# Attention scores of a decoder kernel as eight products of 32 rows and 64 queries in two waves of four, with the keys spread by ScalarE

## The reference

```python
sim = einsum('bghnd,bhsd->bghns', q, k) / scale          # attn0
scores = einsum('bhqd,bhkd->bhqk', Q, K) / sqrt(hd)      # attn1
scores = where(causal, scores + slopes * rel, -inf)
u = einsum('hbqd,hbkd->hbqk', q, k) * scale / sqrt(d_k)  # cross1
logits = tanh(u) * exp(log_C)
```

## Time and profile before

| | us |
|---|---|
| median of 3 runs | 2997.16 (2996.25 to 3002.15) |
| the profiled execution, its own time | 3003.07 |
| span of the profiled execution | 3001.2 |
| TensorE busy (matmul) | 2651.9 (88% of the span) |
| VectorE busy | 2357.9 (79%) |
| ScalarE busy | 1901.2 (63%) |
| GpSimd busy | 1133.4 (38%) |
| mean granted TensorE clock | 0.939 of full speed |

### The profile page before, as it was taken

One profiled execution on the slowest core, in us unless ns is written; L12 is line 12 of the kernel. 1 busy time (PEld: TensorE's weight loads), 2 busy tenths in 40 slices (PEclk: granted clock), 3 DMA queues, 4 the chain that ended last, 5 costly groups with the idle time before them and its releaser, 6 DMA issues.

```text
span 3001.2 us, 97587 instructions
## 1 busy us (share of the span) xinstructions
PE 2651.9 (88%) x36618; PEld 1996.7 (67%) x36618; DVE 2357.9 (79%) x6371; ACT 1901.2 (63%) x3499; POOL 1133.4 (38%) x965
## 2 busy tenths in 40 slices
PE   2999953867888888888899998999989999999998
PEld 2666632546777777777566665666767777777776
DVE  7999999777899999998699998666676666666665
ACT  1777752545566666665466665666667777777776
POOL 0333344008899999998233222444230000000000
PEclk9999975977999999999899999999789999999999
DMA  5000000000000000000100000000000000000000
GB/s 160 1 0 0 0 15 0 1 0 3 1 0 0 0 0 0 0 0 0 58 0 0 0 0 3 16 16 16 7 1 1 1 14 0 0 14 0 14 0 14
DMA packets 28702, 26.67 MB, mean 9 GB/s; under 512 B 4304, under 2 KB 23504, under 8 KB 28496
## 3 DMA queue, kind: packets, MB, share of 16 engines
q1 hardware_dynamic: 28624, 25.63, 2.9%
HBM read 21.43 MB, written 4.19 MB: 9 GB/s over the span
## 4 chain that ended last, share of the span: by engine, by line
PE 82%; DVE 9%; issue 5%; DVEq 1%; ACT 1%; POOL 1%; DMA 0%; ACTq 0%; POOLq 0%; SPq 0%
PE ps L1070 8%; PE ps L896 8%; PE ps L1059 5%; PE ps L1186 5%; PE ps L919 4%; PE ps L934 4%; PE ps L907 4%; PE ps L1084 4%; PE ps L1188 4%; PE ps L1155 4%; PE ps L1187 4%; PE ps L1157 4%; PE ps L1156 4%; DVE work L1612 3%; PE ps L947 2%
## 5 line engine op out<-in xcount | busy, mean ns | idle before, releaser
L470 POOL TENSOR_TENSOR work<-work,consts_sb 128x1024 f32<-128x1024 f32 x192 | 365.0, 1901 | 751.2 <-ACT work L602 590.1
L1070 PEld LDWEIGHTS ps<-work 32*32 32x32 f32 x16384 | 244.0, 145 | 122.9 <-issue 121.2
L1070 PE MATMUL ps<-work 32*32 32x32 f32 x16384 | 249.8, 226 | 72.6 <-DVE work L1612 59.5
L1755 DVE TENSOR_TENSOR h_low<-consts_sb,h_up 128x1024 fp32r<-128x1024 f32 x128 | 158.2, 1236 | 188.2 <-ACT h_up L797 188.2
L722 ACT ACTIVATE ps<-work 128x128 f32<-128x128 f32 x512 | 154.6, 354 | 232.0 <-DVE work L1594 220.9
L896 PE MATMUL ps<-work 128*128 128x512 f32 x512 | 262.4, 614 | 3.1 <-issue 0.2
L1186 PE MATMUL ps<-h_low,d_up 128*128 128x512 f32 x512 | 214.4, 419 | 0.6 <-DVE h_low L1755 0.5
L1155 PE MATMUL ps<-a_low,w_up 128*128 128x512 f32 x512 | 203.4, 397 | 0.9 <-DVE a_low L1730 0.9
L1188 PE MATMUL ps<-h_up,d_low 128*128 128x512 f32 x512 | 200.4, 391 | 0.0
L1157 PE MATMUL ps<-a_up,w_low 128*128 128x512 f32 x512 | 200.4, 391 | 0.0
L1156 PE MATMUL ps<-a_up,w_up 128*128 128x512 f32 x512 | 200.3, 391 | 0.0
(11 more groups left out here) (270 smaller groups left out, 6889.8 us busy)
## 6 DMA issues: line engine op xcount, KB each, us to landing
ctxT_all<-in_ctxT SPq DMA_DIRECT2D x1, 4096.0 KB, 12.9
work<-in_ctx SPq DMA_DIRECT2D x64, 64.0 KB, 1.8
out<-x_all SPq DMA_DIRECT2D x4, 1024.0 KB, 5.1
big<-in_up SPq DMA_DIRECT2D x1, 2048.0 KB, 8.4
consts_sb<-in_consts SPq DMA_DIRECT2D x1, 936.0 KB
w<-in_key_inT SPq DMA_DIRECT2D x1, 512.0 KB, 3.9
w<-in_key_out SPq DMA_DIRECT2D x4, 128.0 KB, 4.0
rows_sb<-in_rows SPq DMA_DIRECT2D x1, 384.0 KB
```

The costliest lines, as they stand in the source:

```text
L470: pool.tensor_tensor(KX[:, u].rearrange("p g (h k) -> p g h k", h=PER_SET), KC[:, u].unsqueeze(2).to_broadcast([P, SETS, PER_SET, SEQ]), o ...
L1070: ins = pe.matmul(psW[rows, n // 16, :, n % 16], XT[rows, T.u, :, n], YT[rows, T.u, :, n], start=True, stop=True)
L1755: dve.tensor_tensor(h_low[:, n], hid[n], h_up[:, n].bitcast(F32), ALU.subtract).then_inc(h_split, 1)
```

## The change

The 128 channels are now four strips of 32 rows with four heads each. A score product takes one strip's 32 rows and the 64 queries of one sequence, against 256 columns: four heads by 64 keys, where `KX[:, u, j, :]` is k with all but head j of each strip zeroed. `quarter_scores` issues four of them as a wave; wave 0 takes strips 0 and 2, wave 1 strips 1 and 3, so that two strips with the same output partitions write banks 0 and 1; wave 1 waits for a semaphore that wave 0 raises. The queries are one plain [128, 128] block (`QT`) with no zero blocks. q and k are each one product of 128 columns, q is copied in one piece, and `spread_k` makes `KX` on ScalarE straight from PSUM in four passes whose scale and bias columns are `own` (1 for the pass's head, else 0) and `own_bk`. GpSimd spreads only in cross1, half as many columns. In attn0 the bias of v enters by two products of one row, and ScalarE copies v; in attn1 VectorE still does. In cross1 the queries are turned by one transpose and copied by VectorE, and the keys are copied from the turned context that is in SBUF already (`cT`). Banks are dealt out anew, the order lists of the three stages are rewritten, and the statistics of x wait on a semaphore in place of a drain.

```diff
-        QB = carve(2 * SETS * P).rearrange("p (u g c) -> p u g c", u=2, g=SETS)
-        KC = carve(2 * SETS * SEQ).rearrange("p (u g k) -> p u g k", u=2, g=SETS)
-        KX = carve(2 * HEADS * SEQ).rearrange("p (u g n) -> p u g n", u=2, g=SETS)
+        QT = carve(2 * P).rearrange("p (u c) -> p u c", u=2)
+        KT = carve(2 * P).rearrange("p (u c) -> p u c", u=2)
+        KX = carve(2 * PER_ROWG * P).rearrange("p (u j c) -> p u j c", u=2, j=PER_ROWG)
...
-        psA, psOT = bank(4, 0), bank(4, P)
-        psQ = bank(4, 2 * P, SETS * SEQ).rearrange("p (g c) -> p g c", g=SETS)
-        psKc = bank(5, 0, SETS * SEQ).rearrange("p (g c) -> p g c", g=SETS)
-        psKd = bank(2, 0, SETS * SEQ).rearrange("p (g c) -> p g c", g=SETS)
-        psV, psY = bank(6, 0), bank(6, P)
+        psA = bank(4, 0)
+        psQ = dict(attn0=bank(4, P), attn1=bank(5, 0))
+        psK = dict(attn0=bank(5, 0), attn1=bank(6, P), cross1=bank(5, 0))
+        psV = dict(attn0=bank(6, 0), attn1=bank(6, 0))
+        psY = dict(attn1=bank(4, P), cross1=bank(6, 0))
+        psOT = dict(attn1=bank(7, 2 * P), cross1=bank(4, 0))
```

The spreading, before and now:

```diff
+            def spread(T):
+
+                pool.wait_ge(aT_ready, T.now(NORM["cross1"]))
+                need(pool, sT_done, T.before(2))
+                pool.tensor_tensor(KX[:, T.u], KT[:, T.u].unsqueeze(1).to_broadcast([P, PER_ROWG, P]),
+                                   own[:, :].unsqueeze(2).to_broadcast([P, PER_ROWG, P]), ALU.mult).then_inc(kx_ready, 1)
...
+            def spread_k(name):
+                base = ATTN[name]
 
                 def seg(T):
                     act.wait_ge(k_done, T.now(base))
-                    need(act, kx_ready, T.before(2, base))
-                    for g in range(SETS):
-                        ins = act.activation(KC[:, T.u, g, :], psKc[:, g, :], ACT.Identity, bias=bk_s[:, g:g + 1])
...
-            def copy_q(base):
+                    need(act, s_done, T.before(2, base))
+                    for j in range(PER_ROWG):
+                        ins = act.activation(KX[:, T.u, j, :], psK[name], ACT.Identity, scale=own[:, j:j + 1], bias=own_bk[:, j:j + 1])
+                    ins.then_inc(kx_ready, 1)
+                return seg
+
...
+                    need(act, s_done, T.before(2, base))
+                    act.activation(QT[:, T.u, :], psQ[name], ACT.Identity, bias=bq_s[:, 0:1]).then_inc(qb_ready, 1)
+                return seg
...
+                    for h in range(2):
+                        part = slice(SEQ * h, SEQ * h + SEQ)
+                        ins = act.activation(VBp[part, T.u, :, :, h, 0:DH], psV[name][part, :].rearrange("p (b i d) -> p b i d", b=2, i=PAIRS),
+                                             ACT.Copy)
+                    ins.then_inc(vb_ready, 1)
+                return seg
```

TensorE:

```diff
+                    if name == "attn1":
+                        pe.wait_ge(kx_ready, T.ahead(1, base, NT))
+                    pe.sem_inc(pe_seen, 1)
+                    if bias is not None:
+                        for h in range(2):
+                            side = slice(SEQ * h, SEQ * h + SEQ)
+                            pe.matmul(to[side, :], ones[SEQ * h:SEQ * h + 1, 0:SEQ], bias[SEQ * h:SEQ * h + 1, :], start=True, stop=False)
                     for b in range(2):
                         for h in range(2):
-                            ins = pe.matmul(psV[SEQ * h:SEQ * h + SEQ, SEQ * b:SEQ * b + SEQ], aT[:, T.u, SEQ * b:SEQ * b + SEQ],
-                                            w[:, SEQ * h:SEQ * h + SEQ], start=True, stop=True)
+                            ins = pe.matmul(to[SEQ * h:SEQ * h + SEQ, SEQ * b:SEQ * b + SEQ], aT[:, T.u, SEQ * b:SEQ * b + SEQ],
+                                            w[:, SEQ * h:SEQ * h + SEQ], start=bias is None, stop=bias is None or b == 1)
                     ins.then_inc(v_done, 1)
...
+            def rows_of(g):
+                return slice(BLOCK * g, BLOCK * g + BLOCK)
+
+            def quarter_scores(u, wave, start):
+
+                at = PER_ROWG * SEQ * wave
+                for n in range(SETS):
+                    for b in range(2):
+                        rows, part = rows_of(SETS * n + wave), slice(SEQ * b, SEQ * b + SEQ)
+                        ins = pe.matmul(ps[part, n, at:at + PER_ROWG * SEQ].rearrange("p (j k) -> p j k", j=PER_ROWG), QT[rows, u, part],
+                                        KX[rows, u, :, part], start=start, stop=start or wave == 1)
+                return ins
+
+            def scores(base, causal, wave):
+
+                def seg(T):
+                    if wave == 0:
                         pe.wait_ge(qb_ready, T.now(base))
                         pe.wait_ge(kx_ready, T.now(base))
-                    need(pe, less_max, T.step(SETS, g + 1 - SETS, base))
-                    if causal:
-                        pe.matmul(ps[:, g, :], maskq_b[0:MASK_ROWS, :], maskk_b[0:MASK_ROWS, g, :], start=True, stop=False)
-                    pe.matmul(ps[:, g, :], QB[:, u, g, :], KX[:, u, g, :], start=not causal, stop=True).then_inc(s_done, 1)
-                return seg
-
-            def scoresT(base):
-
-                def seg(T):
-                    u = T.u
-                    pe.wait_ge(qb_ready, T.now(base))
-                    pe.wait_ge(kx_ready, T.now(base))
-                    need(pe, tanh_done, T.before(1))
-                    for g in range(SETS):
-                        ins = pe.matmul(psST[:, g, :], QB[:, u, g, :], KX[:, u, g, :], start=True, stop=True)
-                    ins.then_inc(sT_done, 1)
+                        need(pe, less_max, T.step(SETS, 0, base))
+                        pe.sem_inc(pe_seen, 1)
+                        if causal:
+                            for n in range(SETS):
+                                pe.matmul(ps[:, n, :], maskq_b[0:MASK_ROWS, :], maskk_b[0:MASK_ROWS, n, :], start=True, stop=False)
+                        quarter_scores(T.u, wave, not causal).then_inc(s_half, 1)
+                    else:
+                        pe.wait_ge(s_half, T.now(base))
+                        pe.sem_inc(pe_seen, 1)
+                        quarter_scores(T.u, wave, not causal).then_inc(s_done, 1)
+                return seg
```

The lists as they are now, of ScalarE, then TensorE, then VectorE, each for attn0, attn1 and cross1:

```diff
-            staggered(nc, act, NT, [(1, copy_aT(NORM["attn0"], v_done, b0)), (4, copy_probsT(b0, 0)), (1, copy_k(b0)),
-                                    (4, copy_probsT(b0, 1)), (1, copy_q(b0)), (3, exps(b0))])
+            staggered(nc, act, NT, [(1, copy_aT(NORM["attn0"], v_done, b0)), (2, spread_k("attn0")), (3, copy_v("attn0")),
+                                    (4, copy_probsT(b0, 0)), (1, copy_q("attn0")), (4, copy_probsT(b0, 1)), (3, exps(b0))])
...
+            staggered(nc, act, NT, [(5, copy_oT("attn1")), (1, copy_aT(NORM["attn1"], v_done, b1)), (4, copy_probsT(b1, 0)),
+                                    (4, copy_probsT(b1, 1)), (1, spread_k("attn1")), (3, exps(b1)), (1, copy_q("attn1"))])
...
+            staggered(nc, act, NT, [(2, tanhs), (4, copy_oT("cross1")), (2, bounded_exps)])
...
+            staggered(nc, pe, NT, [(3, project_v("attn0", n0, small[:, WV0, :], R("bv0"))), (2, project_k("attn0", n0, wk0_s)),
+                                   (3, scores(b0, False, 0)), (3, scores(b0, False, 1)), (1, transposed_beside_q(b0, n0)),
+                                   (5, values_of_pairs(b0)), (4, probsT(b0, 0)), (1, project_q("attn0", n0, wq0_s)), (4, probsT(b0, 1))])
...
+                (3, project_v("attn1", n1, small[:, WV1, :], None)), (3, scores(b1, True, 0)), (5, outputT("attn1", n1)),
+                (3, scores(b1, True, 1)), (1, transposed_beside_y(b1, n1)), (4, probsT(b1, 0)), (4, probsT(b1, 1)),
+                (1, project_q("attn1", n1, wq1_s[:, :])), (1, project_k("attn1", n1, wk1_s[:, :])),
+                (5, out_project("attn1", lambda u: OT[:, u, :], small[:, WO1, :])), (4, values_of_pairs(b1))])
...
+                pe.transpose(psK["cross1"], xn[:, T.u, :], ident).then_inc(aT_raw, 1)
...
+                (2, scoresT(b2, 0)), (1, place_q), (2, scoresT(b2, 1)),
+                (5, out_project("cross1", lambda u: OT[:, u, :], small[:, WOUT, :])), (4, outputT("cross1", n2)), (3, values_of_heads(b2))])
...
+            staggered(nc, dve, NT, [(3, maxima(b0, 0)), (3, maxima(b0, 1)), (3, less_maxima(b0, 0)), (3, less_maxima(b0, 1)),
+                                    (5, normalised(b0, None)), (0, quantised_rows), (5, output_stats)])
...
+            staggered(nc, dve, NT, [(5, normalised(b1, OUTT["attn1"])), (1, normed_rows(NORM["attn1"])), (6, stats_of_sum("attn1")),
+                                    (3, place_v(b1, R("bv1"))), (3, maxima(b1, 0)), (3, maxima(b1, 1)), (3, less_maxima(b1, 0)),
+                                    (3, less_maxima(b1, 1)), (5, add_output("attn1", R("bo1")))])
...
-                ins.then_inc(qb_ready, 1)
+                dve.tensor_copy(QT[:, T.u, :], cTt[:, T.t, :]).then_inc(qb_ready, 1)
...
```

(2 more changed lines are left out.)

216 lines of the change are left out of this document (89 added, 127 removed).

## The result

| | before | after |
|---|---|---|
| median, us | 2998.22 (2996.25 to 3002.15, 4 runs) | 3343.20 (3341.98 to 3345.51, 4 runs) |
| ratio after : before | | 1.115, 95% interval 1.113 to 1.116 |
| the profiled execution, own time / span | 3003.1 / 3001.2 | 3343.6 / 3342.0 |
| mean granted TensorE clock | 0.939 | 0.814 |

A forecast was written before the change was run, and what follows sets the result against it. TensorE's queue was taken to bound the three stages. Savings a tile of 0.45 us (attn0), 0.73 (attn1) and 0.99 (cross1), times 64 tiles, give 139 us: 2858 us forecast, range 2795 to 2950.

The forecast's parts named there:

- What bounds the kernel: In attn0, attn1 and cross1, stages last as long as TensorE's queue; removing work gains time until another engine or wait is longer.
- serial strips: Score strips running one after another in part or whole: rival 1, chance 0.10, and four in turn, chance 0.02.
- The wave: Four score products of 32 rows and 256 columns run all at once, 0.43 us a wave; none at once, 1.71.
- rival 1: Two score strips sharing output partitions take turns: 0.43 us more a wave, 3023 us in all; chance 0.10.
- four in turn: All four strips of a score wave run one after another: 3.4 us of waves a tile, above 3100 us; chance 0.02.
- Rival 2: Weight loads are not hidden in small score strips: 0.22 us more a wave, 2943 us in all; chance 0.13.
- Half wait and change of shape: On TensorE, wave 1's wait for wave 0, 0.25 us in attn0, and 0.1 us for each change of product shape.
- spread_k: ScalarE's four passes in attn0 and attn1 take 0.36 us each, between bounds of 0.295 and 0.484.
- rival 3: ScalarE's passes do not overlap, 0.48 us each: both rings 0.5 us longer, 2920 us in all; chance 0.12.
- The rings: Waits of project_v on ScalarE's v copy in attn0, 4.94 us a tile, and of v on spread_k in attn1, 5.65.
- the wait on spread_k: In attn1, TensorE idles before project_v until ScalarE's spread_k is done, 0.35 us a tile.
- ScalarE and VectorE: In attn0 ScalarE's work goes from 4.1 to 4.7 us a tile, VectorE's from 5.2 to about 4.6; neither exceeds the ring.

The follow-up runs named there:

- the run with 128 rows: The changed kernel with all 128 rows, in place of 32, in each of its eight score products: 3082.8 us.
- the version with two fillers: The changed kernel with two idle 128 by 128 by 512 products a tile in each of the three stages: 3202.7 us; timed again, 3200.1 to 3332.7 us.

## Why the prediction was wrong, by its own steps

**What bounds the kernel.** "A term taken out of this queue is time gained" is the step that failed. It was read from rows in which TensorE is always at full clock, and all terms of the sum were priced at that clock. The two big score products of a tile were work to be removed, and also what kept all 128 rows at work for 1.92 of 5.40 us. The effect of that on the clock is the term that the sum put at nothing. Without them TensorE's whole queue took 1.7 times as long in attn0 and cross1 as it would have at full clock (8.91 for 5.2, 5.70 for 3.3, below). No rival had it either: all four ask how fast the new products and passes run and how long the rings are, none what the old products did for their neighbours. The only ways to the slower side were serial strips, and their chance was 0.12.

**The wave** at 0.43 us: right to 0.02. Strips with the same outputs and other rows run together (0.41 us saved in each wave against products of all rows), so rival 1 and four in turn are out; the run with 128 rows is what rival 1 would have looked like. Rival 2 wanted 0.22 us more in a wave; 0.11 are there (the next point), and 0.10 are there with 128 rows too (wave 1 starts 1.25 after wave 0, for 0.86 of streaming and 0.25, and the transpose 1.01 after wave 1, for 0.86 and 0.1), so they are not the loads of small strips.

**Half wait and change of shape:** too small. Wave starts are 0.84 apart at full clock, where 0.68 was forecast, and the transpose starts 0.59 after wave 1 (256.80 to 257.39), where 0.53 was. That is 0.22 us a tile, or 0.11 a wave. Another 0.1 a tile lies between the product of k and wave 0: 0.42 (255.54 to 255.96), where 0.32 was counted.

**spread_k** at 0.36 a pass: right. ScalarE's timeline of the changed kernel in attn0 has four passes in 1.50 us, as forecast, and rival 3 falls:

```profile
257.93 1.50 ACT L591 ACTIVATE work<-ps,own_bk,own_of_four 128x128 f32<-128x128 f32 x4
259.30 0.58 ACT L612 ACTIVATE work<-ps 64x128 f32<-64x128 f32 x2
```

**The rings.** In attn0 a wait of 0.1 before project_v had been forecast. At full clock it is there in every second step, too short for the idle column: in the version with two fillers the bias products start 0.73 us behind the turn of probabilities (302.75 to 303.48, below), 0.10 after ScalarE's copy of v ends at 303.38, and 0.61 behind it in the next step. For the rest TensorE's own sum, longer than forecast, is what a tile takes. In attn1 the wait on spread_k is there, 0.59 us in place of 0.35, at 1921.33 above.

**What the change would give at full clock** can be estimated from the runs. attn0: the version with two fillers takes 5.69 us from wave to wave (300.14 to 305.83, below), less 2 x 0.22 is 5.25; the version with 128 rows takes 6.05 (299.64 to 305.69), less 2 x 0.41 is 5.23. Steps differ by some 0.1, and the means over the windows above (5.66 and 6.17) give 5.22 and 5.35. Forecast 4.95.

```profile
300.14 0.66 PE L906 MATMUL ps<-work 32*64 32x256 f32 x8 [0.18 <-PE ps L906]
...
302.75 0.60 PE L951 MATMUL ps<-consts_sb,work 128*128 128x128 f32 x4
303.48 0.43 PE L889 MATMUL ps<-rows_sb,ones 1*64 1x128 f32 x4
...
305.83 0.66 PE L906 MATMUL ps<-work 32*64 32x256 f32 x8 [0.18 <-PE ps L906]
```

attn1: 5.92 in the changed kernel itself. Forecast 5.65. cross1: 4.13 - 2 x 0.41 = 3.31 by the one, 4.58 - 6 x 0.22 = 3.26 by the other. Forecast 3.1. The gain would be (0.16 + 0.46 + 0.8) x 64 = 91 us in place of 139, some 2907 us by this estimate, within the range. No kernel shows it, since nothing here holds the clock up for free. So what the forecast says of the queue at full clock was right but for 48 us, and the effect that it left out was worth 345 + 91 = 436, by this estimate.

**ScalarE and VectorE** in attn0: 282.8 and 246.1 us in 61.5 tiles (last rows of this section), 4.6 and 4.0 us a tile, for 4.7 and 4.6 forecast. GpSimd has nothing there. None of it was worth anything to the end, as forecast.

**The clock in the trace of before.** It spoke for TensorE's pauses. Its longest half-clock stretch is one in which TensorE mostly waits: 28.94 us busy in 119, below, at 0.51. Half clock stood beside pauses, and full clock beside a full queue, in the stages of the earlier trace rows and elsewhere; no row there has a full queue of products with few rows for long. The memory stage has them for a part of each tile: L1070, 32 rows, lasts 3.9 of some 12.2 us (its starts at 1102.39 and 1114.57), and yet the stage has 0.93 of the clock, below. In the changed attn0 the waves are 0.84 + 0.59 = 1.43 of some 5.2 us at full clock, no larger a share, and the stage fell. So the share of few rows does not decide alone; what else in the queue counts was not tried. From the trace of before it could have been a rival with a chance and a price, not more. (Of GpSimd in the earlier trace rows the forecast says a third to 43%; in attn1 it is 29%. Nothing hangs on it.)

```profile
419.00:538.00 119.00, 28.94 (x137) 19.37 (x138) 110.22 (x299) 34.09 (x149) 61.15 (x48) 0.51 0.03 9
...
1070.00:1440.00 370.00, 312.67 (x9404) 280.58 (x9394) 330.21 (x1268) 219.91 (x427) 322.78 (x332) 0.93 0.00 0
```

The Trainium skill (TensorE: Matmul & The Clock Gate, "What's actually happening") says that the clock is set by how busy the engine has been, and gives full clock to a busy one; by that rule too the three stages would have stayed at 2.4 GHz. Here TensorE's records cover 529 of 540 us of attn0, below, nearly all of it at 1.2 GHz, so busy time by the profile is not what the clock answers to.

```profile
80.00:620.00 540.00, 529.06 (x4491) 358.72 (x4484) 246.13 (x608) 282.80 (x671) 0.00 (x0) 0.67 0.00 0
```

## What to carry to other kernels

A big product is not only work, it also keeps the rows of the array busy while it runs. Before big products are cut down on TensorE, ask how much of its time is then spent on products of 32 or 64 rows, and put "the whole stage at half clock" among the rivals, priced at the 1.7 times that TensorE's queue took here. The share does not settle it (the memory stage above held 0.93), so try it early, with fewer rows in the products of the kernel as it is. When a kernel comes out slower after TensorE work was taken away, compare an instruction that the change did not touch first: if it is longer, look at the granted clock before looking for waits, and give the new products full rows in a test version to see whether it comes back.
